# Squared-score attention: scores in bands of 32 array rows, with queries masked into even and odd heads

## What is computed

```
def taylor_exp(x):
    x2 = (x[..., :, None] * x[..., None, :]).reshape(*x.shape[:-1], 16 * 16) / R2
    return jnp.concatenate([ones, x / RRD, x2 / RD], axis=-1)
q, k = 16 heads of 16 features;  v = 16 heads of 64 features
A_qk = jnp.tril(jnp.einsum('bhnd,bhmd->bhnm', taylor_exp(q), taylor_exp(k)))
y = jnp.einsum('bhnm,bhme->bhne', A_qk, v)
rms = jax.lax.rsqrt(jnp.mean(y * y, axis=-1, keepdims=True) + RMS_EPS)
out = (y * rms * g_weight).reshape(b, l, 16 * 64) @ Wo.T
x = _layernorm(x + out)
```

## Time and profile before

| | us |
|---|---|
| median of three runs | 1366.65 |
| lowest and highest of the three | 1365.92, 1375.88 |
| the profiled execution | 1375.38 |
| its span | 1373.6 |
| TensorE busy in the span | 1092.5 (80%) |
| VectorE busy | 692.9 (50%) |
| ScalarE busy | 581.6 (42%) |
| mean granted clock of TensorE | 0.894 of full |

### The profile page before, as it was taken

How to read it: one execution, slowest core, us unless ns; L and a number is a source line. 1 busy time by engine, 2 the same in 40 slices (tenths; PEclk the granted TensorE clock), 3 DMA queues, 4 the chain that set the end, 5 groups by cost and what they waited for, 6 DMA issues and landing times.

```text
span 1373.6 us, 20562 instructions
## 1 busy us (share of the span) xinstructions
PE 1092.5 (80%) x8144; PEld 762.3 (56%) x8144; DVE 692.9 (50%) x1616; ACT 581.6 (42%) x1349; POOL 277.6 (20%) x282
## 2 busy tenths in 40 slices
PE   6988588776776787879999768787888486778996
PEld 3676356554446776435565456565666254453764
DVE  3323456632654774364655337575775445636203
ACT  4311146651244653334444325444554144447542
POOL 2401213100040000521111210020001634124443
PEclk9966769988787999899999989999999788789998
DMA  8410324500465770642221046633430000000000
GB/s 295 101 24 0 92 61 102 113 10 0 161 213 184 243 305 13 216 131 84 96 93 62 23 140 229 189 91 91 111 93 1 0 1 1 1 1 1 1 1 27
DMA packets 66591, 123.61 MB, mean 90 GB/s; under 512 B 11536, under 2 KB 42224, under 8 KB 62416
## 3 DMA queue, kind: packets, MB, share of 16 engines
q1 hardware_dynamic: 63728, 117.48, 28.2%
q0 software_dynamic: 1536, 3.67, 0.9%
q10 hardware_dynamic: 1232, 1.15, 0.3%
HBM read 86.30 MB, written 35.92 MB: 89 GB/s over the span
## 4 chain that ended last, share of the span: by engine, by line
PE 54%; DVE 21%; ACT 13%; POOL 4%; DMA 4%; issue 4%; SPq 0%; DVEq 0%; ACTq 0%
PE psum L369 42%; ACT s_p L2214 4%; DVE s_p L2260 2%; POOL rs L2647 2%; DVE s_max L1249 2%; DMA values<-s_v 2%; PE psum L1106 2%; PE psum L1134 2%; DVE s_max L2249 2%; PE psum L2179 1%; PE psum L2168 1%; DVE wu L1079 1%; DVE wd L1079 1%; PE psum L1886 1%; PE psum L2458 1%
## 5 line engine op out<-in xcount | busy, mean ns | idle before, releaser
L592 POOL TENSOR_TENSOR rstd<-meanvar,minus_half 112x1 f32<-112x1 f32 x40 | 23.4, 586 | 527.9 <-DVE meanvar L573 527.8
L2214 ACT ACTIVATE s_p<-psum,s_max 112x375 f32<-112x375 f32 x128 | 72.3, 569 | 78.4 <-DVE s_max L2249 78.4
L1249 DVE TENSOR_REDUCE s_max<-psum 112x2 f32<-112x750 f32 x64 | 60.0, 937 | 38.0 <-PE psum L1106 37.1
L369 PE MATMUL psum<-Wv,ctx 128*125 128x512 f16 x240 | 64.5, 429 | 8.0 <-ACT s_v L552 3.9
L2249 DVE TENSOR_REDUCE s_max<-psum 112x1 f32<-112x375 f32 x128 | 63.7, 539 | 0.9 <-PE psum L2160 0.9
L369 PE MATMUL psum<-ctx,Wk 128*128 128x375 f16 x320 | 61.5, 331 | 1.9 <-DVE s_k L582 1.5
L1198 ACT ACTIVATE s_pT<-psum 125x672 f32<-125x672 f32 x64 | 46.8, 731 | 36.0 <-PE psum L1122 34.7
L369 PE MATMUL psum<-x_ch,w_Wq 128*128 128x224 f32 x192 | 49.6, 395 | 15.3 <-DVE s_q L2236 7.5
L2957 POOL TENSOR_TENSOR hidden<-raw,hidden 128x448 f16<-128x448 f32 x44 | 46.7, 1061 | 64.5 <-ACT hidden L2840 62.9
L2533 ACT ACTIVATE sc<-psum,mx 112x112 f32<-112x112 f32 x128 | 34.5, 358 | 59.2 <-DVE mx L2602 59.1
L552 ACT ACTIVATE s_v<-psum 125x512 f32<-125x512 f32 x48 | 28.4, 597 | 72.8 <-PE psum L369 47.8
(11 more groups left out here) (352 smaller groups left out, 2638.3 us busy)
## 6 DMA issues: line engine op xcount, KB each, us to landing
keys<-s_k SPq DMA_DIRECT2D x64, 187.5 KB, 2.2
s_k<-keys SPq DMA_DIRECT2D x8, 1500.0 KB, 8.1
values<-s_v SPq DMA_DIRECT2D x48, 224.0 KB
s_v<-values SPq DMA_DIRECT2D x16, 672.0 KB
raw_wg<-in_wg SPq DMA_DIRECT2D x8, 1024.0 KB, 5.0
raw_wu<-in_wu SPq DMA_DIRECT2D x8, 1024.0 KB, 5.5
...
```

Source lines behind the costliest of these rows:

```text
L369: ins = TE.matmul(bank, left, right, start=i == 0, stop=last)
L1249: VE.tensor_reduce(s1_max[b % 2][:, 2 * p:2 * p + 2], rings["s1"][unit][0:N, :, 0:S], X, ALU.max, negate=True).then_inc(*V.up("max1", n))
L2214: SC.activation(rings["p4"][2 * n + j], rings["s4"][(n, j)][0:N, 0:S], ACT.Exp, bias=s4_max[b % 2][:, h:h + 1], accum_out=s4_sum[b % 2][:, ...
```

## The change

The queries are no longer copied eight times but twice: `parity`, a new constant of two columns, keeps the even heads in one copy and the odd heads in the other. A product over 32 array rows then sees two heads' features, of which the mask leaves one; the four bands of 32 rows hold the eight heads of a block. An S unit is now four products of 32 rows and 224 columns (both copies of the queries): bands 2q and 2q+1 of block 0 and then of block 1, the even bands into one bank, the odd ones into another. There are two S units for each sequence where there were four, and each takes two banks of `misc3`. ScalarE and VectorE have as many squares and masks as before, two behind each S. A Y unit r now takes the four heads of band r, two of each block, so that every Y unit writes both banks of `y3`; both are taken before the first Y of a sequence, and both are copied (yE) after the last.

```
-    s3_q = [work.tensor(f"s3_q{i}", [P, KC, HPT, 2, N]) for i in range(2)]
+    s3_q = [work.tensor(f"s3_q{i}", [P, KC, 2, 2, N]) for i in range(2)]
...
-    step("s3", "T s3, A sq3, V half3", "misc3", "A sq3", 1200)
+    step("s3", "T s3a, T s3b, A sq3a, A sq3b, V half3a, V half3b", "misc3", "A sq3a", 1500)
...
-        for g in range(6):
-            if g < 4:
-                rings["a3"].take((b, g), (T, ("y3", b, g)))
-                yield [("s3", b, g)]
-                yield next(keys4, None)
-            if g >= 2:
-                if g % 2 == 0:
-                    rings["y3"].take((b, (g - 2) // 2), (A, ("y3", b, (g - 2) // 2)))
-                yield [("y3", b, g - 2)]
-                yield next(keys4, None)
-                if g % 2:
-                    yield [("y3e", b, (g - 2) // 2)]
-            else:
-                yield None
+        for q in range(2):
+            for r, half in ((2 * q, "half3a"), (2 * q + 1, "half3b")):
+                rings["a3"].take((b, r), (T, ("y3", b, r)))
+            rings["misc3"].take(("s3b", b, q), (A, ("sq3b", b, q)))
+            yield [("s3", b, q)]
+            yield next(keys4, None)
+            yield next(keys4, None)
+        for c in range(KC):
+            rings["y3"].take((b, c), (A, ("y3", b, c)))
+        for r in range(4):
+            yield [("y3", b, r)]
+            yield next(keys4, None)
+        for c in range(KC):
+            yield [("y3e", b, c)]
...
-                mm(rings["misc3"][unit][0:N, 0:4 * N],
-                   [(s3_k[j][:, c, b % 2, :], s3_q[j][:, c, h0:h0 + 4, b % 2, :])], T.up("s3", b, g))
+                for c in range(KC):
+                    for i, key in enumerate((unit, ("s3b", b, q))):
+                        r = 2 * q + i
+                        ins = TE.matmul(rings["misc3"][key][0:N, c * 2 * N:(c + 1) * 2 * N],
+                                        s3_k[j][32 * r:32 * r + 32, c, b % 2, :],
+                                        s3_q[j][32 * r:32 * r + 32, c, :, b % 2, :], start=True, stop=True)
+                        if c == KC - 1:
+                            ins.then_inc(*T.up(("s3a", "s3b")[i], b, q))
...
-                act.wait_ge(T["y3", b, 2 * j + 1])
+                act.wait_ge(T["y3", b, 3])
...
-                    rings["misc3"][unit][:, 0:2 * N].unsqueeze(1).to_broadcast([P, HPT, 2 * N]),
-                    headq[:].unsqueeze(2).to_broadcast([P, HPT, 2 * N]),
+                    rings["misc3"][unit][:, 0:2 * N].unsqueeze(1).to_broadcast([P, 2, 2 * N]),
+                    parity[:].unsqueeze(2).to_broadcast([P, 2, 2 * N]),
```

56 lines of the change are left out of this document (32 added, 24 removed).

## The result

The changed kernel took 1350.84 us (median of four runs, 1348.81 to 1356.05) against 1367.1 us (four runs, 1365.92 to 1375.88): a ratio of 0.987, with a 95% interval of 0.983 to 0.991, so 16.3 us less (15.8 below the 1366.65 that the prediction started from). The prediction of 1351.7 us, 15.0 less, was right. Faster by over 1% was also the side of the forecast itself, though the prediction's chances gave that side 0.45 and "within 1%" 0.50; and the interval, which ends at 0.991, does not quite rule out a gain of just under 1%. How far the prediction was right for its reasons is the subject of what follows.

What follows compares the result with a forecast made beforehand. TensorE's own work bounds the stage's middle, the last sequences' chain its end. Work saved less new waits starts the next stage 18.6 us sooner; less 3.6 allowed, 15.0 off the 1366.65 median gives 1351.7 us, range 1344 to 1366.

Steps and rivals of the forecast that it cites:

- Part 1: Scores on TensorE: bands overlap, a new S takes 0.90 us, at most 1.65; all S 9.5 us less.
- (a): Scores: bands don't overlap in fp32, S takes 1.65 us; gain only 3 us, 1363.6 us; chance 15%.
- (c): Scores: a band's weights can't load under its own passes, 11.5 us more; gain 3.5, 1363.2 us; chance 5%.
- (d): Scores: banded S lose all overlap of streams and loads, 3.1 us each; slower, 1386.7 us; chance 5%.
- Part 2: VectorE's narrower query copies: yE ready before T everywhere, so 3.2 us of TensorE's short waits in the middle go.
- Part 3: Stage's start: more units ahead of sequence 0's T, reached at about 617.3 us without waiting; 1.4 us of slow clock gone.
- Part 4: Stage's middle: new TensorE waits for tE, late in ScalarE's row, 9.0 us in sum over sequences 2 to 7.
- Rival (b): Middle: ScalarE's row sets the pace, waits half as much again, four clock falls; gain 7.5, 1359.2 us; chance 20%.
- Rival (e): Middle: the count of new waits is too high and no clock fall comes; gain 19 to 22 us; chance 10%.
- Part 5: Stage's end: last Y at 763.1 us, next stage at 788.8 instead of 807.45, 18.6 us sooner.
- signs of being wrong on the whole: S over 1.2 us, middle waits over 15 us in sum, or last Y to next stage longer than 26 us.
- The allowance: Taken off the gain: 3.6 us, for two clock falls of 1.5 each and 0.6 for missed waits.

Runs made afterwards that it cites:

- e8: Changed kernel with all four products of an S unit on the array's first 32 rows, so none can overlap; one run, 1367.6 us.
- e3: Changed kernel with the queries copied eight times again, banded scores kept; 1359.58 us, ratio 0.9924 to the kernel before.
- e2: Changed kernel's order of units with the old score products and query copies; 1370.57 us, ratio 0.9995 to the kernel before.
- e4: Changed kernel with ScalarE's copy tE placed right behind its t; 1343.67 us, ratio 0.982 to the kernel before.
- second profile: Changed kernel unedited, profiled again; median 1353.27 us, ratio 0.988 to the kernel before.
- e10: Changed kernel with old scores and copies, tE right behind t, sequence 6's O held until sequence 7's mean square is issued; 1355.52 us, ratio 0.985.

## Why the prediction was right

**Part 1, the scores.** 0.94 to 0.95 us for each S against the 0.90 taken; 16 times 0.05 is 0.8 us too little. Bounding from two neighbours with the array divided in other ways came out near the truth, and e8 shows the upper bound was right as well (1.70 against 1.65). What was slightly small is the rest over four steps, 0.15 taken and 0.2 measured. Rivals (a), (c) and (d) fall. On (c): the Trainium skill (TensorE: Matmul & The Clock Gate, Part 3, The mechanism) lets a weight load overlap only across row groups. In e8_one_band all eight passes and loads are in one row group, and they take 1.70, eight passes of 0.187 and a rest of 0.2. Its loads fill 1.40 us from the same start, 0.17 each, so they run under the passes; under none of them they would have added 1.4 us. The trace disagrees with the rule, as Y's rows did.

**Part 2, the copies.** I took 3.2 us of short waits as gone. e3 puts the copies at 3.6 us in the stage and 1.2 ahead of it. The 3.2 did go from the middle: no T waits there, and of its 9.1 us of idle time 8.8 are for tE. But the reason given, "in the new order yE is ready before T everywhere", failed: with the new order and wide copies T waits 6.3 us (e3) and 8.1 (e2), so it is the cheap copy that keeps yE early, and where even that did not do (T of sequence 0) there is a wait. The 1.2 us ahead of the stage are not in the prediction.

**Part 3, the start.** This is the step that was wrong. I had T of sequence 0 at 31.7 us after the first v (617.3 less 585.60) with no wait; TensorE was there at 31.4, but T came at 33.5, after 2.06 us of waiting. ScalarE, changed kernel:

```profile
603.94 0.48 ACT L545 ACTIVATE s_k<-psum 128x375 f16<-128x375 f32 x1 [2.56 <-DMA keys<-s_k]
605.57 0.36 ACT L1928 ACTIVATE s_k<-psum 128x224 f32<-128x224 f32 x1 [1.15 <-DVE s_q L1988]
605.82 0.54 ACT L1950 ACTIVATE s_o<-psum 128x448 f32<-128x448 f32 x1
```

The K copy still waits for its transfer (2.56 us, 3.72 before). Counted from the first v it comes 1.1 us later than before (31.0 against 29.9), so "that transfer does not move" was not quite so either. Behind it stands now the copy of the keys, which waits for VectorE's copy of the queries, and that stands behind VectorE's own part of the same K unit (604.46); behind the keys stands the yE. From the K copy to T it was 0.97 us and is 2.47. I had moved TensorE's units past the wait but not ScalarE's and VectorE's. The 1.4 us that I counted for the clock behind that wait did come: it is at 1.00 from 606 us on. But ahead of T the lower clock lasted from 588 to 595 us, 3.5 us before (604.6 to 608.1), so the start as a whole lost about as much as before.

**Part 4, the new waits.** 9.0 us predicted for the middle, 8.8 in the rows that wait for tE. The single ones differ: sequence 2 has 1.55 and 1.01 where I had one of 1.6; sequences 3 to 6 have one of 1.01 each against 1.15 and 1.4; sequence 7 has 0.60 and 1.50 against 0.8 and 1.5. The sum agrees partly by luck. e4 shows that their cause was named rightly: with tE moved up they all go. Rival (b) had its waits at half as much again; it falls for the waits, but not for the falls of the clock (below). Rival (e) falls as well: the count was not too high, though in the first profile no new fall came.

**Part 5, the end.** From the first T to the last Y I had 145.8 us (617.3 to 763.1); it took 145.5 (606.41 to 751.95). From the last Y to the next stage 25.7, measured 26.3: O is at 5.2 instead of 4.2 and the last T at 8.7 instead of 7.7, and from that T on the chain is 17.6 us, 18.1 before. With 26.3 us, and 27.9 in the second profile, one of the prediction's own signs of being wrong on the whole ("longer than 26 us") came true. It was set only 0.3 us above the forecast of that term, less than two profiles of one kernel differ by; the two other signs (S over 1.2 us, waits in the middle over 15) stayed far off.

**The allowance.** 3.6 us for two falls of the clock and for missed waits. In the first profile neither new fall came. The last O took 5.09 us where 3.46 is its price at the full clock, but that fall is already in the 17.45 us of the chain before, whose last O took 5.81. The stage had 2.1 us more than the sum without the allowance (below): 1.8 from Part 3, 0.6 from Part 5, 0.3 less in the middle. In the repeat two new falls came, at 626 to 637 and 746 to 749 us, and the falls together cost 7.6 us more than in the first profile. The kernel before lost 2.5 us more in its repeat as well, so what the allowance has to meet is the gain in the mean of both pairs, 14.6 us; by that its size was right. A single profile it does not fit: the first lies 1.5 us below the sum with the allowance, the second 5.4 above.

**The sum.** 203.2 us from the first v to the next stage before the allowance, 205.3 measured in the first profile, 212.2 in the second. Against the kernel before: 14.6 us in the mean of both pairs and 1.2 ahead, beside the 15.0 predicted. By parts, the chain of experiments is before, e2 (new order), e3 (banded scores as well), after (narrow copies as well); less the lost time their stages are 212.3, 211.8, 203.9 and 199.6 us. So the order is worth 0.5, the scores 7.9 (8.8 by price: 16 times two old S of 0.75 less one new of 0.95), the copies 4.3 and the 1.2 ahead of the stage: 13.9 in sum, each part good to about 1 us, since repeats differ by 0.6 and 0.7. The ratios go the same way (1, 0.9995, 0.992, 0.987 and 0.988). The rest up to the 14.9 and 16.3 measured fits the clock. The prediction had 9.5 for the scores and 3.2 for the copies, and 18.6 less 9.5, 3.2 and 3.6, so 2.3, for order and clock together: the scores a little too high, the copies too low by 2.3, and the sum right partly by luck. The order pays once the tE and the last O stand right: e10, with the old scores and copies, is 17.0 us shorter in the stage than the kernel before, 12.4 to 13.0 less the lost time. Subtracting from the median and not from the profiled execution was right: that execution held 7 us ahead of the stage that its repeat did not.
